# A recommendation network on one core: gathers without releases, three crossed tiles instead of four, a wait ahead of each one-hot, and fewer loads

## The chip, the cores and the metric

The kernel runs on one core of one Trainium2 chip. The metric is the device time of one execution, in microseconds (us). The kernel before takes 118.74 us, the median of three runs (118.56 to 119.22). The names of the engines are those of the profile: PE is TensorE's matmul, PEld its weight load, DVE is VectorE, ACT is ScalarE, POOL is GpSimd, SP is SyncE, which issues loads and stores here.

## The reference

For 2048 samples there are 13 dense numbers and eight indices. A wide part sums single weights, a deep part is a network of two hidden layers over eight embeddings of 64 numbers and a projection of the dense numbers. Cut to what matters:

```python
VOCABS = [125000, 25000, 12500, 375, 375, 1000, 500, 100]
wide = dense @ Wd_wide
for si, wi in zip(S, w):
    wide = wide + wi[si]
wide = wide + wc0[S[3] * VOCABS[4] + S[4]]
wide = wide + wc1[S[5] * VOCABS[6] + S[6]]
deep_in = concatenate([dense @ Wd_deep] + [Ei[si] for Ei, si in zip(E, S)], axis=1)
h = relu(deep_in @ W1)          # 576 -> 512
h = relu(h @ W2)                # 512 -> 256
deep = h @ W3                   # 256 -> 1
return bias + deep + wide
```

## The kernel before

**Tiling.** The samples are 16 tiles of 128, in four blocks (0 to 3) of four tiles, 512 samples each. Every float32 product with a weight is made of three matmuls on high and low parts (lines L891, L892, L893), so that layer 1 and layer 2 are most of PE's work.

**Two ways to fetch a row.** The three large tables (fields 0, 1, 2) are gathered: POOL issues one indirect DMA for each field and tile, into `x_pair` (fields 0 and 1, 32 gathers) and `x_two` (field 2, 16 gathers), and PE turns the rows over (`turn`, L856). The five small tables lie in SBUF. For them DVE builds a one-hot of each chunk of 128 rows (`build_onehot`, L556: 19 chunks a block, 128x512, float16 index against a row number, into `onehot`), and PE multiplies it with the table (`look_up`, L832) and with its single weights (`look_up_wide`, L844). The indices of a block come spread over all partitions: block 0 by matmuls, blocks 1 to 3 by a DMA (`idx_bc`, L323) from a copy stored in DRAM (`idx_dram`).

**The crossed weights.** `wc1` is gathered for all 16 tiles. `wc0` has 375 x 375 entries, and is gathered for the tiles from `XTILES` on, with 12 gathers (28 in all, `cross`, L388). For the first `XTILES` = 4 tiles PE multiplies a one-hot of the row with the table of 375 rows (`look_up_crossed`, L883, six matmuls of 376 columns), and DVE picks the column (`take_crossed`, L671). The table CROSSED says in which block and place each of these tiles stands on PE.

**Order.** Each engine's order is written by hand, and all waits are semaphores. PE's results of lookups, turns and crossed tiles go round three PSUM banks in the order of the list `IO_ORDER`; a use waits for the engines that empty the use three places earlier. POOL waits ahead of every gather but the first four (`gather_released`): PE counts its work in matmuls of 512 columns and releases gather after gather, one each 5.6 of them for the first eight, then one each 5.85 (`count`, `release_at`). Behind the 48 row gathers POOL issues the 28 of `cross`.

**The start.** SP issues the index, then tables and parts of W1, `look_w` (the single weights of the small tables), the dense numbers, the store of the indices, two parts of W1 and, once the store has landed, the spread of block 1. Behind that stand four small loads (`w3`, `bias`, `dense_s`, `wd_bc`) and then W2, whose buffer `w2_sb` is a part of `w1_sb`: it waits for the spread of block 1 and for `w1_low` (L334 to L337). ACT makes the high part of W2 (L484) ahead of `wide_looked(0)` and the lookups of block 1, and DVE its low part (L562) between the one-hots (1, 0) and (1, 1). Here and below (b, i) is block b and small table i. On PE the order there is `look_up(1, 0)`, `dense(0)`, `turn(0, 0)`, `look_up(1, 1)`, then the last part of block 0's layer 1 and layer 2.

**The end.** The last block's layers end on PE with L1000 and L1009. DVE adds the crossed weights once the last gather has landed (L784, L785), adds the last sums of PE (L788), and SP stores the result.

## Time and profile before

| | us |
|---|---|
| median of three runs | 118.74 |
| the profiled execution | 117.59 |
| its span, first to last instruction | 115.8 |
| PE busy in it | 110.4 |
| POOL busy in it | 84.7 |
| DVE busy in it | 73.1 |
| ACT busy in it | 57.2 |

The profile is of one execution, on one core. The span leaves out 1.8 us of that execution's time that lie around the instructions. Times in the rows below are from the span's start. An engine's busy time counts its instructions, not its issue of DMAs, except on POOL, where the making of a gather's descriptors is shown as an instruction (DMA_INDIRECT). Matmuls overlap, and the duration of one contains its passage through the array: two that follow each other start about 0.23 us apart, though each is shown with 0.39 us.

### The profile page before, as it was taken

How to read it: one execution, taken by the hardware profiler on the slowest of the kernel's cores; microseconds unless marked ns; L12 is line 12 of the kernel's file. 1: busy time of each engine (PE TensorE's matmuls, PEld its weight loads, DVE VectorE, ACT ScalarE, POOL GpSimd, SP SyncE). 2: the span in 40 equal slices, each digit the busy share in tenths (PEclk: the TensorE clock that was granted, in tenths of full speed). 3: DMA queues.
4: the chain of work that ended last, by engine and by line, in shares of the span. 5: the costliest groups of instructions: out<-in, count | busy, mean ns of one | idle time of the engine just before them, and what ended most of it. 6: DMA issues, size and time to landing. Idle time of an engine off the chain costs nothing.

```text
span 115.8 us, 1680 instructions
## 1 busy us (share of the span) xinstructions
PE 110.4 (95%) x572; PEld 85.2 (74%) x572; DVE 73.1 (63%) x186; ACT 57.2 (49%) x105; POOL 84.7 (73%) x87
## 2 busy tenths in 40 slices
PE   5999999979999999999999999999999999999980
PEld 2747685847787885888888886888888886888980
DVE  3699999287999955974992043992993024609211
ACT  5699992288785262249092251339273260426220
POOL 7574777765777977796777767777786777777750
PEclk9999999999999999999999999999999999999997
DMA  2798858348941143202335342320000000000000
GB/s 58 238 228 236 220 92 218 70 28 231 412 75 18 12 82 28 25 6 21 25 23 81 27 32 23 32 19 0 0 0 0 6 1 3 0 1 0 0 0 3
DMA packets 6168, 7.46 MB, mean 64 GB/s; under 512 B 2844, under 2 KB 3868, under 8 KB 6160
## 3 DMA queue, kind: packets, MB, share of 16 engines
q0 software_dynamic: 2432, 1.62, 17.2%
q1 hardware_dynamic: 3728, 5.74, 15.8%
q8 instruction: 4, 0.07, 0.2%
q14 instruction: 4, 0.03, 0.1%
HBM read 7.32 MB, written 0.03 MB: 63 GB/s over the span
## 4 chain that ended last, share of the span: by engine, by line
PE 72%; DMA 16%; SPq 4%; ACT 2%; POOL 2%; issue 1%; DVE 0%; DVEq 0%
PE l_ps L891 16%; PE l_ps L893 16%; PE l_ps L892 15%; PE io_ps L832 11%; DMA w_sb<-in_w_dram 5%; DMA idx_bc<-idx_dram 4%; DMA idx_dram<-row_idx 4%; PE io_ps L883 4%; PE io_ps L844 3%; PE l_ps L961 2%; DMA cross<-in_wc_dram,idx_cross 2%; PE io_ps L856 2%; POOL cross L388 2%; PE io_ps L986 2%; SPq L296 1%
## 5 line engine op out<-in xcount | busy, mean ns | idle before, releaser
L378 POOL DMA_INDIRECT x_pair<-in_rows_dram,idx_gather x32 | 35.2, 1100 | 12.3 <-issue 7.0
L388 POOL DMA_INDIRECT cross<-in_wc_dram,idx_cross x28 | 27.8, 992 | 8.5 <-issue 4.6
L556 DVE TENSOR_SCALAR onehot<-idx_bc,row_id 128x512 fp32r<-128x512 f16 x76 | 31.7, 482 | 2.2 <-PE io_ps L844 2.0
L378 POOL DMA_INDIRECT x_two<-in_rows_dram,idx_gather x16 | 19.6, 1228 | 5.9 <-issue 3.0
L891 PE MATMUL l_ps<-xt_hi,w_hi 128*128 128x512 f32 x56 | 22.3, 398 | 0.0
L893 PE MATMUL l_ps<-xt_hi,w_lo 128*128 128x512 f32 x56 | 22.0, 393 | 0.0
L892 PE MATMUL l_ps<-xt_lo,w_hi 128*128 128x512 f32 x56 | 21.9, 392 | 0.0
L832 PE MATMUL io_ps<-onehot,table_hl 128*128 128x512 f32 x76 | 21.2, 408 | 0.4 <-ACT xt_lo L417 0.4
L832 PEld LDWEIGHTS io_ps<-onehot,table_hl 128*128 128x128 f32 x76 | 14.1, 188 | 5.5 <-DVE onehot L556 1.6
L416 ACT CAST xt_hi<-io_ps 64x512 fp32r<-64x512 f32 x20 | 11.6, 579 | 12.0 <-PE io_ps L832 11.8
L610 DVE SCALAR_TENSOR_TENSOR h_lo<-l_ps,h_hi 128x512 fp32r<-128x512 f32 x16 | 10.1, 686 | 8.8 <-ACT h_hi L437 8.8
L446 ACT ACTIVATE h<-l_ps 128x512 f32<-128x512 f32 (+2 forms) x10 | 5.0, 512 | 19.3 <-PE l_ps L893 19.3
L891 PE MATMUL l_ps<-h_hi,w_hi 128*128 128x512 f32 (+1 forms) x36 | 13.4, 372 | 0.0
L893 PE MATMUL l_ps<-h_hi,w_lo 128*128 128x512 f32 (+1 forms) x36 | 13.3, 368 | 0.0
L892 PE MATMUL l_ps<-h_lo,w_hi 128*128 128x512 f32 (+1 forms) x36 | 13.2, 366 | 0.0
L891 PEld LDWEIGHTS l_ps<-xt_hi,w_hi 128*128 128x128 f32 x56 | 10.5, 188 | 2.7 <-issue 0.4
L577 DVE TENSOR_TENSOR xt_lo<-io_ps,xt_hi 128x512 fp32r<-128x512 f32 x4 | 2.8, 692 | 15.0 <-ACT xt_hi L430 15.0
L893 PEld LDWEIGHTS l_ps<-xt_hi,w_lo 128*128 128x128 f32 x56 | 10.5, 188 | 2.3
L892 PEld LDWEIGHTS l_ps<-xt_lo,w_hi 128*128 128x128 f32 x56 | 10.5, 188 | 2.3
L417 ACT CAST xt_lo<-io_ps 64x512 fp32r<-64x512 f32 x20 | 11.7, 583 | 0.5
L437 ACT ACTIVATE h_hi<-l_ps 128x512 fp32r<-128x512 f32 x16 | 8.7, 602 | 3.9 <-PE l_ps L893 3.6
L891 PEld LDWEIGHTS l_ps<-h_hi,w_hi 128*128 128x128 f32 x36 | 6.8, 189 | 1.4 <-issue 0.4
(106 smaller groups left out, 129.3 us busy)
## 6 DMA issues: line engine op xcount, KB each, us to landing
idx_bc<-idx_dram SPq DMA_DIRECT2D x3, 640.0 KB, 8.1
w_sb<-in_w_dram SPq DMA_DIRECT2D x4, 256.0 KB, 5.6
dense_x<-in_dense_x_dram SPq DMA_DIRECT2D x4, 154.0 KB
table<-in_wc_rows_dram SPq DMA_DIRECT2D x1, 564.0 KB, 6.0
x_pair<-in_rows_dram,idx_gather POOLq DMA_INDIRECT x32, 3.4
w_sb<-in_w_dram SPq DMA_DIRECT2D x1, 512.0 KB, 6.3
cross<-in_wc_dram,idx_cross POOLq DMA_INDIRECT x28, 2.4
x_two<-in_rows_dram,idx_gather POOLq DMA_INDIRECT x16, 3.6
```

What stands on the lines that cost most here:

```text
L378: nc.gpsimd.indirect_dma_start(out=x_two[:, t // 2, t % 2 * ROW:(t % 2 + 1) * ROW] if f == 2 else x_pair[:, t, f * ROW:(f + 1) * ROW], out ...
L388: nc.gpsimd.indirect_dma_start(out=cross[:, c, t:t + 1], out_offset=None, in_=wc[c], in_offset=bass.IndirectOffsetOnAxis(ap=idx_cross[:, c ...
L416: nc.scalar.copy(xt_hi[b % 2][to, g, :], bank[0:D, :]).then_inc(io_act, 1)
L417: nc.scalar.copy(xt_lo[b % 2][to, g, :], bank[D:2 * D, :]).then_inc(io_act, 1)
L437: nc.scalar.activation(h1_hi[:, m, :], l1_ps[m][:], ACT.Relu).then_inc(l1_high, 1)
L446: nc.scalar.activation(h2[:, m, s], l2_bank(part)[:, s], ACT.Relu).then_inc(h2_ready, 1)
L556: nc.vector.tensor_scalar(onehot[:, CHUNK0[i] + c, :], idx_bc[:, b % (BLOCKS - 1), i, :], row_id[:, c:c + 1], None, ALU.is_equal).then_inc ...
L610: nc.vector.scalar_tensor_tensor(out=h1_lo[:, m, :], in0=l1_ps[m][:], scalar=0.0, in1=h1_hi[:, m, :].bitcast(f32), op0=ALU.max, op1=ALU.su ...
L832: last = count(nc.tensor.matmul(io_bank(use)[:], table_hl[:, c, :], onehot[:, c, :], start=c == CHUNK0[i], stop=ends), free=not ends)
L891: count(nc.tensor.matmul(dst, w_hi, a_hi, start=start, stop=False), columns, free=True)
L892: count(nc.tensor.matmul(dst, w_hi, a_lo, start=False, stop=False), columns, free=True)
L893: return count(nc.tensor.matmul(dst, w_lo, a_hi, start=False, stop=stop), columns)
```

## The change

What it does:

- POOL waits for no release; PE counts no work and sends none.
- `XTILES` is 3: one crossed tile less on PE (that of block 2, ahead of `look_up_wide`) and on DVE, one matmul less in `spread_row`, and row one-hots of 384 columns where they had 512. POOL issues 29 gathers of `cross`, 77 in all.
- In `build_onehot`, DVE waits in blocks 1 to 3 ahead of each one-hot until the one before it is finished.
- In block 0 `look_up(0, 4)` comes ahead of `turn(0, 1)`, on PE and on ACT, and in IO_ORDER.
- `look_w`, `w3`, `bias`, `wd_wide` and `dense_s` come as one load, `few`, in the place of `look_w`.
- W2 has a buffer of its own, comes in rows of 4 KB laid out ahead, and is issued right behind the spread of block 1, without waits.

```diff
-XTILES = 4
+XTILES = 3
-PACE, FIRST_PACE, PACED_FROM = 5.85, 5.6, 9
-FIRST_RELEASED = BT * 2
-RELEASED = FIRST_RELEASED + (BLOCKS - 1) * BT * NG + NX * TILES - XTILES
-CROSSED = {(1, 3): [0], (2, 1): [1], (2, 3): [2], (3, 1): [3]}
+CROSSED = {(1, 3): [0], (2, 3): [1], (3, 1): [2]}
-IO_ORDER = [("look", 0, i) for i in range(4)] + [("turn", 0, 1), ("look", 0, 4), ("wide", 0, 0)]
+IO_ORDER = [("look", 0, i) for i in range(4)] + [("look", 0, 4), ("turn", 0, 1), ("wide", 0, 0)]
...
+        few = sb("few", [P, sum(FEW)], f32)
-        w2_sb = w1_sb[:, 2:4, :].rearrange("p g n -> p (g n)").rearrange("p (k n) -> p k n", n=H2)
+        w2_sb = sb("w2_sb", [P, M1, H2], f32)
...
-            sp.dma_start(look_w[:], small_w).then_inc(look_w_loaded, 16)
+            sp.dma_start(few[:], few_in).then_inc(few_loaded, 16)
...
             spread_block(1)
-            sp.dma_start(w3_sb[:], w3).then_inc(w3_loaded, 16)
-            sp.dma_start(bias_sb[:], bias.to_broadcast([P, 1])).then_inc(bias_loaded, 16)
-            sp.dma_start(dense_s[:], dense_s_in).then_inc(dense_s_loaded, 16)
-            sp.dma_start(wd_bc[:], wd_wide.to_broadcast([P, ND])).then_inc(wide_weight_loaded, 16)
-            sp.wait_ge(index_spread[1], 16)
-            sp.wait_ge(w1_low, 2)
-            sp.dma_start(w2_sb, w2.rearrange("(k p) n -> p k n", p=P)).then_inc(w2_loaded, 16)
+            sp.dma_start(w2_sb[:].rearrange("p k n -> p (k n)"), w2).then_inc(w2_loaded, 16)
             dense_block(1)
...
                         for f in fields:
-                            if b > 0 or f != 2:
-                                released += 1
-                                pool.wait_ge(gather_released, released)
                             nc.gpsimd.indirect_dma_start(
...
                 for c in every:
+                    if b > 0:
+                        dve.wait_ge(onehot_ready, b * NCH + CHUNK0[i] + c)
                     nc.vector.tensor_scalar(
                         onehot[:, CHUNK0[i] + c, :], idx_bc[:, b % (BLOCKS - 1), i, :], row_id[:, c:c + 1],
                         None, ALU.is_equal).then_inc(onehot_ready, 1)
...
             layer1(0, 2, range(2, M1))
+            look_up(0, 4)
             turn(0, 1)
-            look_up(0, 4)
             layer1_weights_low_last(3)
```

DVE's row in the start of block 1, where the waits for a one-hot come in; line numbers differ between the kernels, as the changed one is shorter. Before:

```order
L556 TENSOR_SCALAR onehot<-idx_bc,row_id 128x512 [waits io_full,index_spread1]
L556 TENSOR_SCALAR onehot<-idx_bc,row_id 128x512 x2
L562 TENSOR_TENSOR w_lo<-w_sb,w_hi 128x1024 [waits w2_high]
L556 TENSOR_SCALAR onehot<-idx_bc,row_id 128x512 x3
L577 TENSOR_TENSOR xt_lo<-io_ps,xt_hi 128x512 [waits io_act]
L556 TENSOR_SCALAR onehot<-idx_bc,row_id 128x512 x2
L610 SCALAR_TENSOR_TENSOR h_lo<-l_ps,h_hi 128x512 [waits l1_high] x4
L556 TENSOR_SCALAR onehot<-idx_bc,row_id 128x512 x3
```

And of the change:

```order
L535 TENSOR_SCALAR onehot<-idx_bc,row_id 128x512 [waits onehot_ready,io_full,index_spread1]
L535 TENSOR_SCALAR onehot<-idx_bc,row_id 128x512 [waits onehot_ready] x2
L541 TENSOR_TENSOR w_lo<-w_sb,w_hi 128x1024 [waits w2_high]
L535 TENSOR_SCALAR onehot<-idx_bc,row_id 128x512 [waits onehot_ready] x3
L556 TENSOR_TENSOR xt_lo<-io_ps,xt_hi 128x512 [waits io_act]
L535 TENSOR_SCALAR onehot<-idx_bc,row_id 128x512 [waits onehot_ready] x2
L587 SCALAR_TENSOR_TENSOR h_lo<-l_ps,h_hi 128x512 [waits l1_high] x4
L535 TENSOR_SCALAR onehot<-idx_bc,row_id 128x512 [waits onehot_ready] x3
```

The order is the same; each one-hot now waits for `onehot_ready`, its predecessor's own signal.

SP's row from `look_w` to the table of crossed weights. Before:

```order
L308 DMA look_w<-in_small_w_dram 128x19
L314 DMA dense_x<-in_dense_x_dram 77x512
L318 DMA idx_dram<-row_idx 80x128 [waits row_index_ready]
L299 DMA w_sb<-in_w_dram 128x512 x2
L323 DMA idx_bc<-idx_dram 128x2560 [waits row_index_stored]
L329 DMA w_sb<-in_w_dram 128x2
L330 DMA bias_sb<-in_bias_dram 128x1
L331 DMA dense_s<-in_dense_s_dram 128x208
L332 DMA wd_bc<-in_wd_wide_dram 128x13
L337 DMA w_sb<-in_w_dram 128x4x256 [waits w1_low,index_spread1]
L314 DMA dense_x<-in_dense_x_dram 77x512 [waits dense_split]
L344 DMA table<-in_wc_rows_dram 128x1128 [waits table_low,rows_gathered0_1,rows_gathered0_0]
```

And of the change:

```order
L298 DMA few<-in_few_dram 128x243
L304 DMA dense_x<-in_dense_x_dram 77x512
L308 DMA idx_dram<-row_idx 80x128 [waits row_index_ready]
L289 DMA w_sb<-in_w_dram 128x512 x2
L313 DMA idx_bc<-idx_dram 128x2560 [waits row_index_stored]
L319 DMA w_sb<-in_w_dram 128x1024
L304 DMA dense_x<-in_dense_x_dram 77x512 [waits dense_split]
L326 DMA table<-in_wc_rows_dram 128x1128 [waits table_low,rows_gathered0_1,rows_gathered0_0]
```

Four loads are gone between the spread (`idx_bc`) and W2 (`w_sb`, the 128x1024 one), with the two waits of W2.

PE's row in block 2, from the end of layer 1's part with pair 3 to `turn(2, 1)`. The name `x_two` marks that turn, `wide_deep_look` the turning of block 1's sums (`turn_deep(1)`). Before:

```order
L883 MATMUL io_ps<-cross_hl,row_onehot 128x376 [waits io_dve,io_act]
L883 MATMUL io_ps<-cross_hl,row_onehot 128x376 x5
L844 MATMUL io_ps<-onehot,look_w_parts 32x512 [waits io_dve,io_act]
L844 MATMUL io_ps<-onehot,look_w_parts 32x512 x18
L986 MATMUL io_ps<-ident,wide_deep_look 128x128 [waits io_dve,io_act,h2_used]
L986 MATMUL io_ps<-ident,wide_deep_look 128x128 x3
L856 MATMUL io_ps<-ident,x_two 128x128 [waits io_dve,io_act,rows_gathered2_1]
L856 MATMUL io_ps<-ident,x_two 128x128
```

And of the change:

```order
L805 MATMUL io_ps<-onehot,look_w_parts 32x512 [waits io_dve,io_act]
L805 MATMUL io_ps<-onehot,look_w_parts 32x512 x18
L943 MATMUL io_ps<-ident,wide_deep_look 128x128 [waits io_dve,io_act,h2_used]
L943 MATMUL io_ps<-ident,wide_deep_look 128x128 x3
L816 MATMUL io_ps<-ident,x_two 128x128 [waits io_dve,io_act,rows_gathered2_1]
L816 MATMUL io_ps<-ident,x_two 128x128
```

The crossed tile (L883, six matmuls) is gone ahead of `look_up_wide` (L844 and L805).

## Rows read from the trace of the kernel before

**Rows 1.** Page, part 1: engine, busy us, share of the span, instructions.
```profile
PE 110.4 (95%) x572; PEld 85.2 (74%) x572; DVE 73.1 (63%) x186; ACT 57.2 (49%) x105; POOL 84.7 (73%) x87
```

**Rows 2.** Busy time by stretch: us, busy us of each engine, granted clock, DMA share.
```profile
50.00:60.00 10.00, 10.00 (x46) 8.31 (x46) 7.61 (x19) 6.33 (x12) 8.17 (x7) 1.00 0.25 18
```

**Rows 3.** Timeline of the end: start us, us, engine, line, what.
```profile
111.88 0.58 PE L1009 MATMUL io_ps<-w_sb,h 128*128 128x1 f32 x4
...
111.07 0.94 POOL L388 DMA_INDIRECT cross<-in_wc_dram,idx_cross  x1 [0.30 <-issue]
...
113.42 0.17 DVE L784 TENSOR_TENSOR wide_cross<-wide_bias,cross 128x16 f32<-128x16 f32 x1 [2.56 <-DMA cross<-in_wc_dram,idx_cross]
...
113.72 0.15 DVE L788 TENSOR_TENSOR result<-wide_cross,io_ps 128x4 f32<-128x4 f32 x1
```

**Rows 4.** Chain of waits, in order of time: start us, us, what.
```profile
10.91 5.20 DMA idx_bc<-idx_dram
...
16.13 6.29 DMA w_sb<-in_w_dram
...
96.14 1.04 PE io_ps L883 x6
...
111.07 2.33 DMA cross<-in_wc_dram,idx_cross
```

**Rows 5.** Timeline of POOL: start us, us, what, idle before and who ended it.
```profile
3.83 1.10 POOL L378 DMA_INDIRECT x_two<-in_rows_dram,idx_gather  x1 [1.13 <-DVE idx_gather L541]
...
9.78 0.98 POOL L378 DMA_INDIRECT x_pair<-in_rows_dram,idx_gather  x1 [0.71 <-PE io_ps L832]
...
12.02 0.99 POOL L378 DMA_INDIRECT x_pair<-in_rows_dram,idx_gather  x1 [1.25 <-PE l_ps L891]
...
26.36 0.94 POOL L378 DMA_INDIRECT x_pair<-in_rows_dram,idx_gather  x1 [0.71 <-PE io_ps L832]
...
28.38 0.94 POOL L378 DMA_INDIRECT x_pair<-in_rows_dram,idx_gather  x1 [1.07 <-PE l_ps L891]
...
37.41 2.87 POOL L378 DMA_INDIRECT x_two<-in_rows_dram,idx_gather  x1 [0.30 <-issue]
...
48.54 3.70 POOL L378 DMA_INDIRECT x_pair<-in_rows_dram,idx_gather  x1 [0.30 <-issue]
...
76.01 1.28 POOL L388 DMA_INDIRECT cross<-in_wc_dram,idx_cross  x1 [0.30 <-issue]
...
106.01 0.94 POOL L388 DMA_INDIRECT cross<-in_wc_dram,idx_cross  x1 [0.30 <-PE l_ps L891]
```

**Rows 6.** Line L556, all its instructions: ns min/median/max.
```profile
L556 DVE TENSOR_SCALAR onehot<-idx_bc,row_id x76: 463/480/589, 4.9 to 85.9; 128x512 fp32r<-128x512 f16 x76
```

**Rows 7.** Timeline of DVE, starts and lengths in blocks 0 to 2.
```profile
32.24 0.19 DVE L536 SCALAR_TENSOR_TENSOR idx_wrap<-idx_pair,vocab 128x32 f32<-128x32 f32 x1
...
32.47 0.21 DVE L538 TENSOR_TENSOR idx_sum<-idx_wrap,idx_pair 128x32 f32<-128x32 f32 x1
...
35.70 3.26 DVE L556 TENSOR_SCALAR onehot<-idx_bc,row_id 128x512 fp32r<-128x512 f16 x8
...
48.17 3.25 DVE L556 TENSOR_SCALAR onehot<-idx_bc,row_id 128x512 fp32r<-128x512 f16 x8
```

**Rows 8.** Timeline of the start, ACT, DVE and PE.
```profile
22.44 1.05 ACT L484 CAST w_hi<-w_sb 128x1024 fp32r<-128x1024 f32 x1 [4.35 <-DMA w_sb<-in_w_dram]
...
23.52 1.23 DVE L562 TENSOR_TENSOR w_lo<-w_sb,w_hi 128x1024 fp32r<-128x1024 f32 x1 [2.67 <-ACT w_hi L484]
...
13.13 0.44 PE L856 MATMUL io_ps<-ident,x_two 128*128 128x128 f32 x2 [0.22 <-DMA x_two<-in_rows_dram,idx_gather]
...
24.21 0.66 PE L856 MATMUL io_ps<-ident,x_pair 128*128 128x128 f32 x4 [0.18 <-DMA x_pair<-in_rows_dram,idx_gather]
...
25.29 1.20 PE L832 MATMUL io_ps<-onehot,table_hl 128*128 128x512 f32 x3 [0.42 <-ACT xt_lo L417]
```

**Rows 9.** Timeline of PE, one lookup of eight chunks.
```profile
39.02 2.02 PE L832 MATMUL io_ps<-onehot,table_hl 128*128 128x512 f32 x8
```

More of the change, by code:

```diff
@@ L146, in program @@
         table_hl = sb("table_hl", [P, NCH, 2 * D], f32r)
-        look_w = sb("look_w", [P, NCH], f32)
+        few = sb("few", [P, sum(FEW)], f32)
+        look_w, w3_sb, bias_sb, wd_bc, dense_flat = (few[:, sum(FEW[:k]):sum(FEW[:k + 1])] for k in range(len(FEW)))
+        dense_s = dense_flat.rearrange("p (t k) -> p t k", k=ND)
         look_w_rest = sb("look_w_rest", [P, NCH], f32)
@@ L368, in _ @@
             pool.wait_ge(gather_index_ready, 1)
-            released = 0
             for b in range(BLOCKS):
@@ L831, in look_up @@
                     ends = c == CHUNK0[i] + CHUNKS[i] - 1
-                    last = count(nc.tensor.matmul(io_bank(use)[:], table_hl[:, c, :], onehot[:, c, :],
-                                                  start=c == CHUNK0[i], stop=ends), free=not ends)
+                    last = nc.tensor.matmul(io_bank(use)[:], table_hl[:, c, :], onehot[:, c, :],
+                                                  start=c == CHUNK0[i], stop=ends)
                 last.then_inc(io_full, 1)
```

105 lines of the change are left out of this document (38 added, 67 removed).

## The prediction, made before the changed kernel was run

> **What bounds the kernel now.** I read the page's first part, the busy time by stretch, the end of the timelines, the chain of waits, and then POOL, DVE and the start one by one. The page has PE busy for 95% of the span [rows 1], and the stretch from 50 to 60 us stands for all from 30 to 110 us: 10.00 of 10.00 us at the full granted clock, 2.4 GHz, while DVE and ACT have room [rows 2]. So whatever PE is spared in the middle comes off PE's end. The end itself is not PE's, though. PE's last matmul ends at 111.88 + 0.58 = 112.46 us, but the last gather, issued at 111.07, lands 2.33 us later, at 113.40 [rows 3, 4]. Only then DVE adds the crossed weights (L784, 113.42), and L788 closes at 113.72 + 0.15 = 113.87 [rows 3]. Two lines of work thus run side by side to the end, PE and POOL, and POOL is behind by 0.9 us. A gain on one alone is cut off by the other.
>
> **POOL's line, today.** From the first gather at 3.83 to the start of the last at 111.07 are 107.24 us for 75 steps [rows 3, 5]. An undisturbed step is 0.94 us of work and 0.30 us between, as at 106.01 [rows 5]; 75 of them are 93.0 us. The idle time before a gather that PE released is more than 0.30 in four places worth counting: 0.71, 1.25, 0.71 and 1.07 us, in sum 2.54 us over [rows 5]. After 30 us POOL hardly ever waits for a release: it runs behind them. What is left, 107.24 - 93.0 - 2.5 = 11.7 us, is gathers longer than 0.94 us. Two of them have 1.93 and 2.76 us of it (2.87 and 3.70 us, at 37.41 and 48.54), and both lie in a run of eight one-hots on DVE (35.70 to 38.96 and 48.17 to 51.42) [rows 5, 7]. In other such runs a gather is late by 0.34 us at most, as at 76.01 [rows 5]. So a gather can be kept out by one-hots that follow each other without a gap.
>
> **Releases gone, one gather more.** The removed waits give POOL 2.5 us, all of it ahead of 30 us, and the 77th gather costs 1.24 us. With the 11.7 us unchanged the last gather would start at 3.83 + 76 x 1.24 + 11.7 = 109.8, land at 112.1 and let DVE end 0.47 us later, at 112.6. That is 1.3 us before today's 113.87. For the gathers themselves being early does no harm: every one has its own place in `x_pair`, `x_two` or `cross`.
>
> **The wait ahead of each one-hot.** Today one takes 480 ns (463 to 589) [rows 6], and a run of eight takes 3.26 us [rows 7], so they start (3.26 - 0.48) / 7 = 0.40 us apart and overlap by 0.08. The trace has no one-hot that waits for its predecessor, but steps that do: L536 starts at 32.24 and takes 0.19, L538 starts at 32.47 [rows 7], 0.04 us after its end. So I take 0.48 + 0.04 = 0.52 us a one-hot, 0.12 us more. The bounds are 0 and 0.19 us (0.589 instead of 0.48, and the 0.04). Waits behind another instruction of DVE find the one-hot long finished and are free; 46 of the 57 follow a one-hot, so DVE does 5.5 us more in 80 us, and it has room. What is queued behind is the rest of DVE: low parts, row one-hots, the sums. PE waits for the one-hots themselves. The tightest place is (1, 4): 35.70, earlier by the 1.3 us below and later by three paid waits (0.37), is 34.8; the eighth one-hot is done at 34.8 + 0.48 + 7 x 0.52 = 38.9. PE's eighth matmul of that lookup, started today at 39.02 + 7 x 0.23 = 40.6 [rows 9], would want it at 39.3. So 0.4 us of cover are left there, and over 1 us at (2, 1) and (3, 1). I cost it at nothing for PE, and at 0.5 us as the outer bound.
>
> What it buys is the gap between two one-hots. If a stuck gather comes through with 0.34 us in place of 1.93 or 2.76 us, the two give 4.0 us back. Then POOL's line ends at 112.6 - 4.0 = 108.6. The bounds are 0 (the gap of 0.04 us is not enough) and 4.7 us. I take 4.0, since every other run of eight has its gathers at 0.34 us or less even without gaps. The Trainium skill (SBUF — State Buffer, in "SBUF: two separate sides") says of this that DVE and GpSimd take a shared pair of SBUF ports as an exclusive lock for a whole instruction, and that a software-made DMA then waits for its descriptors. The two long gathers agree with it; the other gathers in such runs, longer by 0.34 us at most, show that POOL needs the ports for a small part of its 0.94 us.
>
> **The crossed tile on PE.** Six matmuls of 376 columns: 1.04 us in the chain for one tile [rows 4], at full clock in a stretch with nothing idle. It was the only work between layer 1 and `look_up_wide` in block 2, and block 1 has gone without one there without a wait. The spread of three rows and not four spares one small matmul, about 0.05 us. Together 1.1 us off PE.
>
> **The start.** W2 is issued at 16.13 and is there 6.29 us later [rows 4]. ACT waits 4.35 us for it, and DVE 2.67 us for ACT [rows 8]; behind DVE's 1.23 us stand the one-hots (1, 1), so that PE starts `look_up(1, 1)` after an idle 0.42 us and gets its one-hots 0.40 apart (the record puts it to ACT, but DVE's first one-hot is what ends then). From the turn at 24.21 to the end of the lookup, 25.29 + 1.20 less the 0.16 us of passage, are 2.12 us for work of 1.15 (four half-size transposes 0.45, three matmuls 0.70). If W2 is there by 19, DVE makes the low part and the one-hots (1, 1) before PE gets there, and 0.95 us go. W2 is now issued at about 11.4, behind the spread of block 1 alone; its 6.29 us would end at 17.7, and up to 1.5 us later if the two share the engines. Next late is then the high part of `turn(0, 0)` on ACT, for 0.1 us. The wait of 0.22 us for `x_two` at 13.13 goes, because the lookup comes first, and its eight one-hots end soon enough; the wait of 0.18 us for `x_pair` at 24.21 [rows 8] goes, because the block's gathers are 0.41 + 0.95 us earlier [rows 5]. In all 0.95 + 0.22 + 0.18 - 0.1 = 1.25, say 1.3 us. Bounds: 0 and 1.6. `few` has the place of `look_w` and is some 120 KB where that was 10, which delays what is behind it by a few tenths; the first user of either comes at 15 us, and nothing of it is near.
>
> **The sum.** PE's last matmul ends at 112.46 - 1.1 - 1.3 = 110.1, DVE's L788 at 110.3, with POOL's line at 108.6 out of the way. Today's is 113.87: 3.6 us less, against the profiled execution's own 117.59 (span 115.8) a time of 114.0. The runs' median is 1.15 us above that execution. I take the difference over to it and round down: 118.74 - 3.5 = 115.2.
>
> **Rivals.**
> 1. POOL stays the bound. The gaps are too short, and the 11.7 us stay, or others get stuck in the 4.1 us runs. It decides as soon as those losses are above 110.3 - 100.9 = 9.4 us. With all of them the end is 112.6 and the time 118.74 - 1.3 = 117.4. For it speaks how short 0.04 us is, against it that most gathers in such runs pass even today with no gap at all. The last gather's landing would then end the chain again, PE being done 1 to 2 us before.
> 2. The start gives nothing. The spread of block 1 took 5.20 us with little beside it [rows 4]; with W2 right behind, both could slow down to 11.5 us in sum, W2 then lands at 22.4 as today, and only the crossed tile and POOL's 0.9 us are gained: 118.74 - 2.3 = 116.4. Against it: it takes a queue in which W2 moves only after everything else.
> 3. Slower than before: POOL holds DVE. In the gaps a gather gets in and keeps the next one-hot out for all of its 0.94 us. A run of eight meets three gathers, a run of three two. With a hold h, PE would wait 3h - 0.4 at (1, 4), 2h - 1.2 at (2, 1) and (3, 1) each, and 2h - 0.8 at (1, 1), in sum 9h - 3.6. With h = 0.94 that is 4.9 us and 118.74 - 3.5 + 4.9 = 120.1; it is slower than before from h = 0.79 on. Against it: of 76 one-hots, many of which start in the middle of a gather, none took over 589 ns [rows 6], so h is some 0.1 us. The rule of the Trainium skill named above, that whichever of the two starts first has the ports for the whole instruction, would give this rival if DMA_INDIRECT counted as one such instruction.
>
> **How the numbers follow.** The forecast has 0.60, POOL as the bound 0.18, the start without gain 0.15, DVE held 0.05, anything else 0.02. The range runs from 114.2 (all bounds on the good side: the start 1.6 us, and runs in which POOL was further behind than in the profiled one) to 117.2, which holds the second rival and most of the first. About 0.5%, 0.6 us, is what a measurement can tell from no change. Faster by more than that: 0.91; within it, mostly from the first rival with more losses or the third with a small hold, 0.05; slower 0.04.
>
> **What would show it.** In the profile of the changed kernel: the last gather landed 1 to 2 us before PE's last matmul, and L788's counterpart right behind PE; no gather over 1.5 us in blocks 1 to 3; runs of eight one-hots at 4.1 us; W2's high part on ACT ahead of 20 us, with no idle PE between 13 and 26 us; 18 matmuls with a crossed tile, not 24. Wrong would be a PE that idles ahead of a lookup in block 1 for a one-hot, or a chain that ends in a gather.

## The result, and the profile after

The changed kernel takes **115.02 us** (median of 4 runs, 114.75 to 115.29), the kernel before 118.65 us (median of 4, 117.99 to 119.22). The ratio is 0.970, with a 95% interval of 0.964 to 0.975: faster by 3.6 us, against 3.5 forecast. Here and below a ratio counts only runs within 1.5% of the fastest of their kernel, while medians and ranges count all of them.

The page of the changed kernel, engines and chain (part 1: busy us, share of the span, instructions; part 4: shares of the chain that ended last):

```profile
span 113.5 us, 1658 instructions
...
PE 109.7 (97%) x565; PEld 84.5 (74%) x565; DVE 79.9 (70%) x184; ACT 57.1 (50%) x105; POOL 80.1 (71%) x88
...
PE 91%; ACT 3%; DMA 2%; DVE 1%; issue 1%
```

PE's share is up from 95 to 97%, and DVE has 6.8 us more work than in [rows 1]. Now the end, by the chain of waits (start us, us, what):

```profile
110.13 0.79 PE io_ps L957 x8
110.92 0.46 PE io_ps L967 x4
...
111.41 0.16 DVE result L762
```

and by the tile `cross`, which the last gathers write (the first row gives ns min/median/max and first and last start; the last one the time from issue to landing):

```profile
L364 POOL DMA_INDIRECT cross<-in_wc_dram,idx_cross x5: 940/944/944, 99.2 to 104.2; - x5
...
L758 DVE TENSOR_TENSOR wide_cross<-wide_bias,cross x1: 169/169/169, 109.7 to 109.7; 128x16 f32<-128x16 f32 x1
...
DMA to landing us min/median/max: 2.3/2.4/2.4
```

The last gather is issued at 104.2, not 111.07 [rows 3], and lands by 106.6. DVE adds the crossed weights at 109.7, as soon as it gets to them, and then waits for PE alone. The chain of [rows 4] that ended in a gather is gone. The last operation of DVE starts 0.05 us after PE's last matmul ends (110.78 + 0.58 = 111.36); in [rows 3] it started 1.26 us after. The end moved from 113.87 to 111.41 + 0.16 = 111.57, so this profiled execution (115.29 us) is 2.3 us shorter than the one before (117.59), while the medians are 3.6 us apart. Of the 2.3 us, 1.2 are that POOL is no longer behind, and 1.1 that PE ends earlier. The difference between 2.3 and 3.6 is taken up below.

DVE in blocks 1 and 2, the rows that answer to [rows 7]:

```profile
35.21 4.61 DVE L535 TENSOR_SCALAR onehot<-idx_bc,row_id 128x512 fp32r<-128x512 f16 x8
...
44.95 1.53 DVE L535 TENSOR_SCALAR onehot<-idx_bc,row_id 128x512 fp32r<-128x512 f16 x3 [1.37 <-issue]
...
47.79 4.88 DVE L535 TENSOR_SCALAR onehot<-idx_bc,row_id 128x512 fp32r<-128x512 f16 x8
```

and the line itself, to be held against [rows 6] (ns min/median/max, and who waited for it, us and times):

```profile
L535 DVE TENSOR_SCALAR onehot<-idx_bc,row_id x76: 474/487/697, 4.9 to 85.8; 128x512 fp32r<-128x512 f16 x76
...
who waited for it (us, times):
  PEld io_ps L793: 1.0, 2
```

A run of eight takes 4.6 to 4.9 us, not 3.26. POOL's timeline shows what that buys. These are all the gathers over 1.4 us:

```profile
12.38 1.88 POOL L356 DMA_INDIRECT x_pair<-in_rows_dram,idx_gather  x1 [0.30 <-issue]
...
14.57 1.80 POOL L356 DMA_INDIRECT x_pair<-in_rows_dram,idx_gather  x1 [0.30 <-issue]
...
21.91 1.90 POOL L356 DMA_INDIRECT x_pair<-in_rows_dram,idx_gather  x1 [0.30 <-issue]
...
68.56 1.46 POOL L364 DMA_INDIRECT cross<-in_wc_dram,idx_cross  x1 [0.30 <-issue]
```

The gathers of 2.87 and 3.70 us [rows 5] have no counterpart. The sum of what the gathers take above 0.94 us, called POOL's losses from here on, fell from 11.1 us to 5.5 us. Three of the four above lie ahead of 24 us. Two of these are in block 0, whose one-hots carry no wait. The other two of the four stand beside a single DVE instruction, where a wait between one-hots can't help: the one at 21.91 beside the low part of W2 (21.78, 1.21 us, below), the one at 68.56 beside an operation on `wide_deep_look` (L603, 68.46, 0.74 us). Both gathers end 0.82 us after that instruction does.

The start, rows that answer to [rows 8]:

```profile
12.43 0.43 SPq L319 DMA_DIRECT2D w_sb<-in_w_dram  x1
...
18.53 1.05 ACT L460 CAST w_hi<-w_sb 128x1024 fp32r<-128x1024 f32 x1
...
21.78 1.21 DVE L541 TENSOR_TENSOR w_lo<-w_sb,w_hi 128x1024 fp32r<-128x1024 f32 x1
...
13.45 2.09 PE L793 MATMUL io_ps<-onehot,table_hl 128*128 128x512 f32 x8 [0.33 <-ACT xt_lo L393]
...
24.64 0.94 PE L793 MATMUL io_ps<-onehot,table_hl 128*128 128x512 f32 x3
```

W2 is issued at 12.43 us, an us later than forecast, and early enough: neither ACT nor DVE waits for it any more, and the three-chunk lookup at 24.64 starts without a wait. An idle 0.33 us ahead of the eight-chunk lookup at 13.45 is new.

### The profile page after: what moved, and what is told of

Read it like the earlier page. It is cut to its first block, busy times and chain, and to the rows that moved or that the text cites. A ratio compares the mean times of both kernels' runs of the same rounds, so it can differ in the third digit from the quotient of the medians.

```text
span 113.5 us, 1658 instructions
## 1 busy us (share of the span) xinstructions
PE 109.7 (97%) x565; PEld 84.5 (74%) x565; DVE 79.9 (70%) x184; ACT 57.1 (50%) x105; POOL 80.1 (71%) x88
## 4 chain that ended last, share of the span: by engine, by line
PE 91%; ACT 3%; DMA 2%; DVE 1%; issue 1%
PE l_ps L848 18%; PE l_ps L850 18%; PE l_ps L849 18%; PE io_ps L793 15%; PE io_ps L805 4%; PE l_ps L918 3%; PE io_ps L842 3%; PE io_ps L816 2%; DMA idx_raw<-in_index_dram 2%; PE l_ps L881 2%; PE l_ps L777 2%; PE io_ps L943 2%; ACT xt_lo L393 1%; ACT xt_hi L392 1%; PE l_ps L989 1%; PE l_ps L885 1%
## 5 line engine op out<-in xcount | busy, mean ns | idle before, releaser
L535 DVE TENSOR_SCALAR onehot<-idx_bc,row_id 128x512 fp32r<-128x512 f16 x76 | 39.3, 532 | 5.1 <-issue 2.8
L356 POOL DMA_INDIRECT x_pair<-in_rows_dram,idx_gather x32 | 34.2, 1069 | 9.7 <-issue 9.7
L793 PE MATMUL io_ps<-onehot,table_hl 128*128 128x512 f32 x76 | 20.7, 405 | 0.3 <-ACT xt_lo L393 0.3
L356 POOL DMA_INDIRECT x_two<-in_rows_dram,idx_gather x16 | 15.8, 986 | 5.8 <-issue 4.6
L422 ACT ACTIVATE h<-l_ps 128x512 f32<-128x512 f32 (+2 forms) x10 | 5.0, 512 | 20.2 <-PE l_ps L850 20.2
L848 PEld LDWEIGHTS l_ps<-xt_hi,w_hi 128*128 128x128 f32 x56 | 10.5, 188 | 2.8 <-issue 0.5
L850 PEld LDWEIGHTS l_ps<-xt_hi,w_lo 128*128 128x128 f32 x56 | 10.5, 188 | 2.5
L393 ACT CAST xt_lo<-io_ps 64x512 fp32r<-64x512 f32 x20 | 11.7, 583 | 0.5
L556 DVE TENSOR_TENSOR xt_lo<-io_ps,xt_hi 128x512 fp32r<-128x512 f32 x4 | 2.8, 692 | 11.8 <-ACT xt_hi L406 11.8
```

The source lines that it names most:

```text
L356: nc.gpsimd.indirect_dma_start(out=x_two[:, t // 2, t % 2 * ROW:(t % 2 + 1) * ROW] if f == 2 else x_pair[:, t, f * ROW:(f + 1) * ROW], out ...
L393: nc.scalar.copy(xt_lo[b % 2][to, g, :], bank[D:2 * D, :]).then_inc(io_act, 1)
L422: nc.scalar.activation(h2[:, m, s], l2_bank(part)[:, s], ACT.Relu).then_inc(h2_ready, 1)
L535: nc.vector.tensor_scalar(onehot[:, CHUNK0[i] + c, :], idx_bc[:, b % (BLOCKS - 1), i, :], row_id[:, c:c + 1], None, ALU.is_equal).then_inc ...
L793: last = nc.tensor.matmul(io_bank(use)[:], table_hl[:, c, :], onehot[:, c, :], start=c == CHUNK0[i], stop=ends)
L848: nc.tensor.matmul(dst, w_hi, a_hi, start=start, stop=False)
```

## The experiments

Three questions: which edit gives what, whether edits that look separate depend on each other, and why PE got a little slower per matmul, which nothing in the prediction foresaw. The runs were made in five further sessions on four chips (the second and the fourth session had the same chip), and each kernel is compared with the kernel before in its own session. The changed kernel itself ran in the third alone, so times and traces that are set against it from the fourth and fifth come from different chips. In the first two sessions the kernel before took 129 to 130 us, in the other three about 117. These three come first.

### Both kernels' halves: releases back, waits out, waits alone

Third session. The changed kernel again, as a base for this chip:

> The changed kernel once more, unchanged, beside the kernel before on the same chip. In its first measurement it took 115.0 us against 118.65; on two other chips the kernel before took 129 to 130 us, and every kernel that gathers without releases 184 to 190, PE standing still until POOL's last gather. Theory A, it depends on the chip or its state and on the releases: if the kernel before takes 128 us or more here, this one takes 180 to 190; if the kernel before takes 118 to 119, this one takes 115. Theory B, only the variants had that fault and the change itself does not: 115 to 125 whatever the kernel before takes.

Measured: 115.26 us (114.88 to 115.75), the kernel before 116.80, ratio 0.991 (0.983 to 0.998). The last gather is issued at 104.45, POOL's losses are 6.0 us, DVE's last operation waits for PE at 111.14. So the traces repeat to 0.3 us, but the gain here is 1% (1.1 us by the ratio), not 3%: it is the kernel before that differs between sessions. The kernel before took neither the 118 to 119 us nor the 128 that the first theory has as its conditions; the changed kernel took the 115 us that go with the former.

The changed kernel with the releases of its 73 gathers put back (waits, three tiles and loads kept):

```diff
                         for f in fields:
+                            if b > 0 or f != 2:
+                                released += 1
+                                pool.wait_ge(gather_released, released)
                             nc.gpsimd.indirect_dma_start(
```

> The changed kernel with the releases of the kernel before put back (same count of work, 73 releases), its tiles, waits, order and loads as changed. Theory A, a release keeps POOL from running ahead of a PE that stands still: on a chip where the kernel before takes 128 to 130 us this one takes 122 to 126, not 180; on a chip where that one takes 118.65, this takes 115 to 116, since POOL's 2.5 us of waits are covered by the 4 to 5 us that POOL's line was ahead in the changed kernel's trace. Theory B, another part of the change makes PE stand still: 180 or more here too. Step of PE's matmuls: 0.2295 us if it hangs on the releases, 0.2332 if on another part.

Measured on the same chip: 117.23 us (116.65 to 118.49), level with the kernel before (ratio 1.006, 0.996 to 1.016), and by the two ratios about 1.7 us more than the changed kernel. The expectation, 115 to 116 us with the releases covered, missed. Its PE, POOL and DVE at the end:

```profile
110.84 0.58 PE L997 MATMUL io_ps<-few,h 128*128 128x1 f32 x4
...
110.08 0.94 POOL L377 DMA_INDIRECT cross<-in_wc_dram,idx_cross  x1 [0.30 <-PE l_ps L879]
...
112.56 0.18 DVE L771 TENSOR_TENSOR wide_cross<-wide_bias,cross 128x16 f32<-128x16 f32 x1 [2.71 <-DMA cross<-in_wc_dram,idx_cross]
```

The losses are as low as without releases (5.4 us, a gather of 2.07 us at 33.28 among them), and still the last gather is issued 5.6 us later. PE's last matmul ends at 110.84 + 0.58 = 111.42, 0.3 us later than in the changed kernel beside it (111.10), and DVE's last operation, L775, starts at 112.85, not at 111.46 where PE would let it. So of the 1.7 us between the two profiled executions (116.74 and 115.03) 1.4 are POOL's wait. The step from matmul to matmul stays that of the changed kernel, so it doesn't hang on the releases.

Fourth session. The other half, the kernel before with nothing but the waits:

```diff
                 for c in every:
+                    if b > 0:
+                        dve.wait_ge(onehot_ready, b * NCH + CHUNK0[i] + c)
                     nc.vector.tensor_scalar(
```

> The kernel before with the one-hot waits of blocks 1 to 3 alone, releases and loads kept. Theory (waits open room for POOL's gathers, PE is not held by them): POOL's losses between gathers fall from 11 to about 4.5 us and none is stuck for over 2.2 us in blocks 1 to 3, but the releases, which PE sets at its own pace, still bind the last gather, so it is issued at 110.5 to 111 on an undisturbed chip as before, and the time falls by no more than 1 us against the kernel before. Rival (the stuck gathers were the whole loss): the last gather comes 2 to 4 us earlier and the time is 2 to 3% down, as with the whole change. Second rival (waits hold PE): 1 us slower.

Measured: 116.34 us (115.63 to 118.28), the kernel before 117.70 (115.52 to 121.62, 19 runs), ratio 1.003 (0.995 to 1.010): no change. The losses halve (5.3 us), but the last gather moves by only 2.0 us against the trace of [rows 3], and DVE still waits for it:

```profile
111.19 0.58 PE L1012 MATMUL io_ps<-w_sb,h 128*128 128x1 f32 x4
...
109.04 1.02 POOL L388 DMA_INDIRECT cross<-in_wc_dram,idx_cross  x1 [0.30 <-issue]
...
111.50 0.17 DVE L787 TENSOR_TENSOR wide_cross<-wide_bias,cross 128x16 f32<-128x16 f32 x1 [1.33 <-DMA cross<-in_wc_dram,idx_cross]
```

The theory's part on POOL and on the time both held; the last gather came earlier, by 1.5 us, than the 110.5 to 111 I had expected. Part of that is PE, which sets the releases and reached layer 2 at 28.33 here, 0.9 us earlier than in the other trace. And the wait for the gather costs nothing here: DVE's last operation (L791, 111.81) starts 0.04 us after PE's last matmul ends (111.77). The two lines are level.

And the changed kernel without its waits, on the same chip:

```diff
-                    if b > 0:
-                        dve.wait_ge(onehot_ready, b * NCH + CHUNK0[i] + c)
```

> The changed kernel without its one-hot waits; releases still gone. Prediction's theory: the waits buy 4.0 us of POOL's losses, so here the losses are back near 11 us, with the two stuck gathers; the last gather is issued at about 108 instead of 104.2, lands before PE's last matmul or up to 0.5 us behind it, and the time is 0 to 1 us over the changed kernel's. Rival from the two disturbed chips: gathers that nobody releases let PE stand still while they run, and the waits hide it; then this kernel stands near 185 to 190 us on this chip too, with PE's gaps in the records put down to issue.

Measured: 116.81 us (114.90 to 120.19, 4 runs), too scattered for an interval. The rival, 185 us or more, is out here. Now the profile of the run of 115.63 us. The losses are back at 10.5 us, two gathers are stuck in runs of eight (49.36, 2.01 us and 58.05, 1.68 us) and one (33.27, 2.10 us) beside DVE's low part of `cross_hl`, a single instruction of 1.33 us. POOL is level with PE again at the end:

```profile
111.05 0.58 PE L964 MATMUL io_ps<-few,h 128*128 128x1 f32 x4
...
108.71 1.27 POOL L364 DMA_INDIRECT cross<-in_wc_dram,idx_cross  x1 [0.30 <-issue]
...
111.43 0.17 DVE L755 TENSOR_TENSOR wide_cross<-wide_bias,cross 128x16 f32<-128x16 f32 x1 [1.38 <-DMA cross<-in_wc_dram,idx_cross]
```

DVE's last operation (L759) starts at 111.73, 0.10 us after PE's last matmul ends (111.63), where the changed kernel has 0.05. So in this execution the waits would have bought no more than 0.06 us of time. The four runs took 114.90, 115.63 (the trace), 117.98 and 120.19 us; no trace shows what the last two lost. On an undisturbed chip the waits are thus shown to halve POOL's losses, and not to shorten the time.

The four together, start of the last gather and POOL's losses, each from its profile:

| | no waits | waits |
|---|---|---|
| releases | 111.07, 11.1 us (before, 76 gathers) | 109.04, 5.3 us (76); 110.08, 5.4 us (77) |
| no releases | 108.71, 10.5 us (77) | 104.16, 5.5 us; 104.45, 6.0 us (77) |

Taking 75 or 76 undisturbed steps of 1.24 us and the losses from the whole, what is left is waiting for releases: 107.24 - 93.0 - 11.1 = 3.1 us in the kernel before, 105.23 - 93.0 - 5.3 = 6.9 us with the waits added (first gather at 3.81). In the changed kernel, which has no releases, 0.5 us are left (100.21 - 94.2 - 5.5), so this sum is that much too high. A POOL that loses less only runs into the releases sooner. The waits alone move the last gather by 2.0 us, the releases alone by 2.4, or 3.6 at equal count of gathers; both move it by 8.2 at equal count. The rows come from different chips, and where there are releases PE's own start is in them, so differences of a few tenths say nothing.

### The step from matmul to matmul

Grouped by line and shape, 56 matmuls each (busy us, mean ns of one), the changed kernel:

```profile
L848 PE MATMUL l_ps<-xt_hi,w_hi 128*128 128x512 f32 x56 | 22.5, 402 | 0.0
L849 PE MATMUL l_ps<-xt_lo,w_hi 128*128 128x512 f32 x56 | 22.1, 395 | 0.0
L850 PE MATMUL l_ps<-xt_hi,w_lo 128*128 128x512 f32 x56 | 22.1, 395 | 0.0
```

The same groups of the kernel before:

```profile
L891 PE MATMUL l_ps<-xt_hi,w_hi 128*128 128x512 f32 x56 | 22.3, 398 | 0.0
L893 PE MATMUL l_ps<-xt_hi,w_lo 128*128 128x512 f32 x56 | 22.0, 393 | 0.0
L892 PE MATMUL l_ps<-xt_lo,w_hi 128*128 128x512 f32 x56 | 21.9, 392 | 0.0
```

It is only 2 to 4 ns, but it is in every profile of the changed kernel and its variants, with and without releases, with and without waits, at the same granted clock. Their starts are 0.2332 us apart on the mean, and 0.2295 in those of the kernel before. One candidate is left by the diff: `few` and an own `w2_sb` move every later tile to another SBUF address (`xt_hi`, `xt_lo`, `h1_hi` and `h1_lo` by 3776 bytes a partition, `w1_hi` by -256, `w2_hi` by 3840). So the changed kernel was laid out as before, with gaps (fourth session):

```diff
-        few = sb("few", [P, sum(FEW)], f32)
+        sb("gap_look_w", [P, NCH], f32)
...
+        few = sb("few", [P, sum(FEW)], f32)
+        sb("gap_rest", [P, 40], f32)
         wd_rep = sb("wd_rep", [D, NROWS], f32)
...
-        w2_sb = sb("w2_sb", [P, M1, H2], f32)
...
+        sb("gap_w3_bias", [P, 16], f32)
         x_pair = sb("x_pair", [P, TILES, 2 * ROW], f32)
...
         result = sb("result", [P, TILES], f32)
+        w2_sb = sb("w2_sb", [P, M1, H2], f32)
```

> The changed kernel, with gaps put between its tiles in SBUF so that the operands of the layers and of the one-hot matmuls (one-hots, tables, transposed rows, hidden values, weights) lie at the very addresses that they had in the kernel before; few stands where the dense inputs were and w2_sb behind the last tile. Question: a 512-column matmul of the layers follows the last one after 0.2332 us in every profile of the changed kernel and its variants, and after 0.2295 us in those of the kernel before. Theory A, addresses: the step is back at 0.2295, PE's last matmul comes 1.3 to 1.6 us earlier than in the changed kernel (at about 109.3 instead of 110.8 on an undisturbed chip), and the time is 1 to 1.5 us under that of the changed kernel, unless POOL's last gather then ends it. Theory B, the step hangs on something else of the program (its instructions, its order): 0.233, and the changed kernel's time.

Measured: 114.36 us (114.07 to 115.45, 10 runs; ratio to the kernel before 0.987, 0.981 to 0.992). The groups read:

```profile
L851 PE MATMUL l_ps<-xt_hi,w_hi 128*128 128x512 f32 x56 | 22.3, 398 | 0.0
L853 PE MATMUL l_ps<-xt_hi,w_lo 128*128 128x512 f32 x56 | 22.0, 393 | 0.0
L852 PE MATMUL l_ps<-xt_lo,w_hi 128*128 128x512 f32 x56 | 21.9, 392 | 0.0
```

These are the kernel before's numbers, so the addresses set the step: theory A. What it is worth I had put too high: I had counted 480 matmuls with this step, and the traces have about 250 pairs of layer matmuls that follow each other directly. The stretch from the first matmul of layer 2 to the first of its last group has the same work in both, in the changed kernel

```profile
28.50 0.47 PE L848 MATMUL l_ps<-h_hi,w_hi 128*128 128x512 f32 x1
...
104.34 0.40 PE L848 MATMUL l_ps<-h_hi,w_hi 128*128 128x512 f32 x1
```

and with the old addresses

```profile
27.88 0.47 PE L851 MATMUL l_ps<-h_hi,w_hi 128*128 128x512 f32 x1
...
103.20 0.39 PE L851 MATMUL l_ps<-h_hi,w_hi 128*128 128x512 f32 x1
```

that is 75.84 against 75.32 us. So the addresses cost 0.5 us by this pair. The kernel before takes 105.47 - 29.20 = 76.27 us for the stretch, with one crossed tile more; 76.27 - 1.1 = 75.2, and by that it is 0.65 us. Which tile's address does it was not tried.

### Fewer crossed tiles

Fourth session as well. If PE alone bounds the changed kernel, a tile less on it should give its 1.1 us again:

```diff
-XTILES = 3
+XTILES = 2
-CROSSED = {(1, 3): [0], (2, 3): [1], (3, 1): [2]}
+CROSSED = {(1, 3): [0], (2, 3): [1]}
```

> The changed kernel with two crossed tiles on TensorE instead of three: 78 gathers instead of 77 on POOL, 1.1 us less on PE (12 transposes and matmuls of one tile). Theory (PE bounds the changed kernel alone, POOL has room: its last gather is issued at 104.2 and lands about 3 us before PE's last matmul): PE's last matmul 1.1 us earlier, time 1.0 to 1.2 us (0.9%) under the changed kernel's. Rival (another gather is what ends it): the last gather's landing moves from 106.5 to 107.8, still before PE, so no change or slower only if PE is held by gathers, as on the two disturbed chips, where it would be near 190.

Measured: 114.05 us (113.68 to 114.75; ratio 0.987, 0.978 to 0.996). The stretch of layer 2 (28.10 to 102.97) is 74.87 us, 1.0 less than the 75.87 of the changed kernel run again (28.21 to 104.08). The last gather is issued at 105.65, and DVE adds the crossed weights at 108.33 without a wait. The theory held, both on PE and on POOL; the time is 1.2 us under the changed kernel's of the third session.

Fifth session. Both at once, two tiles and the old addresses:

> The changed kernel with two crossed tiles on TensorE and with the addresses of the kernel before, both at once. Theory (the two gains are independent, both are PE's): the step is 0.2295 us, PE's last matmul comes 1.2 us earlier than with two tiles alone (at about 108.2 instead of 109.41), the last gather is issued at 105.6 and lands at about 108.1 to 108.3, still before it, and the time is 112.6 to 113.0 us on an undisturbed chip, about 1% under each of the two changes alone. Rival (POOL's line is next: its last gather lands at 108.3 and two DVE operations follow it): the gain of both together is cut off and the time stays at 113.4 or above, with DVE's crossed sum waiting for the gather.

Measured: **113.38 us** (113.08 to 114.50, 6 runs), the kernel before 117.29, ratio 0.974 (0.967 to 0.982): the fastest version here, though missing the 112.6 to 113.0 expected. Its rows:

```profile
28.66 0.47 PE L851 MATMUL l_ps<-h_hi,w_hi 128*128 128x512 f32 x1
...
102.89 0.39 PE L851 MATMUL l_ps<-h_hi,w_hi 128*128 128x512 f32 x1
...
108.19 0.17 DVE L761 TENSOR_TENSOR wide_cross<-wide_bias,cross 128x16 f32<-128x16 f32 x1
...
109.92 0.16 DVE L765 TENSOR_TENSOR result<-wide_cross,io_ps 128x4 f32<-128x4 f32 x1 [1.35 <-PE io_ps L970]
```

The stretch of layer 2 takes 74.23 us, 0.64 less than with two tiles alone, so the gains do add. DVE does not wait for a gather, so the rival is out. In the profiled execution (113.80) what is missing was lost ahead of 28.66: it came to layer 2 0.56 us later than the one of two tiles alone. Whether that holds for the other five runs isn't shown.

### Two sessions in which PE stood still

First session, on a chip where the kernel before took 130.09 us (128.06 to 130.70):

> The kernel before once more, unchanged, for a second trace. Its profiled execution took 117.59 us where its unprofiled median is 118.65, and in its trace two layer matmuls start 0.2295 us apart where in the changed kernel's trace they start 0.2332 apart, which over some 480 columns-of-512 matmuls is 1.5 us of the span. Theory A, the step belongs to the execution and not to the program: this trace has a step near 0.2332 and a span near 117. Theory B, the change slows PE (POOL or DVE being busier beside it): this trace has 0.2295 again and a span of 115.8. On POOL's line, the theory of stuck gathers expects two or more gathers over 1.9 us in other places than 37.41 and 48.54, since it is a matter of chance which of them meets a run of one-hots.

> Only one part of the change: the wait ahead of each one-hot of blocks 1 to 3. Theory of two lines (the end is the later of PE's last matmul and the last gather's landing): POOL's losses fall by about 6 us (in the changed kernel's trace they are 5.4, before 11.2), so POOL is no longer behind and PE's last matmul, at 112.5 to 114 depending on the step of its matmuls, ends the chain. The time falls by 0.9 to 1.5 us, to about 117.4. Rival, the waits do nothing for the end because POOL is held back by the releases of PE: 118.6 as before. Rival, the waits cost PE: one-hot runs of eight at 4.8 us delay the lookup (1, 4) and the time rises to 119 or more.

> The changed kernel without the waits ahead of one-hots, all else as changed. Theory of two lines: gathers get stuck again; with POOL's losses at 11 to 12 us its last gather lands at 112 to 113 us, behind PE's 111.4, and the time is 115.6 to 116.8. With another two or three stuck gathers it is more, and it varies more from run to run than the changed kernel's 114.75 to 115.29. Rival, waits are irrelevant and the gain is all PE's (tile, loads): 115.0 or, as DVE is spared 7 us, a little under.

> The changed kernel with one crossed tile on PE in place of three; two gathers more on POOL. Theory of two lines: PE's last matmul comes 2 x 1.04 + 0.1 us earlier, at 109.2, POOL's last gather starts 2 x 1.25 us later, at 106.7, and lands at 109.0. Both lines are even, and the time falls by 2.0 to 2.2 us, to 112.9. Rival, something else sets the end in the changed kernel (DVE's sums, the load of weights): less than 1 us. If POOL loses more than in the changed kernel's trace, it becomes the bound again: 113.5 to 114.

None of the times expected of these four could be tested, since what follows sets every time here. The kernel before measured 129.9 us. Its gathers are stuck beside the same two runs of eight as before (2.87 us at 37.73, 3.69 us at 51.09), where I had expected other places and chance, and its losses are 11.0 us. Its step is 0.2296 us, so the step does not belong to one execution. But its PE stopped for 5.20 us ahead of 78.87 with nothing to wait for. With the waits alone it took 125.59 us (124.99 to 129.64), ratio 0.975 (0.956 to 0.995), losses 4.5 us. Both kernels without releases fell apart: the changed kernel without waits took 188.69 us (183.84 to 189.26), the one with a single crossed tile, waits kept, 189.88 (188.82 to 190.81). Busy time by stretch of the kernel without waits (us; busy us and instructions of PE, PEld, DVE, ACT, POOL; granted clock; DMA share; GB/s):

```profile
60.00:80.00 20.00, 0.00 (x0) 0.00 (x0) 0.00 (x0) 0.51 (x2) 15.12 (x17) 0.50 0.18 13
...
120.00:140.00 20.00, 20.00 (x92) 16.36 (x91) 11.74 (x27) 8.85 (x16) 0.00 (x0) 1.00 0.02 8
```

PE has no instruction on record in 20 us in which POOL issues its gathers at an even pace. The trace puts PE's 26 us of idling ahead of 80.14 down to ACT's L422, and that one waited 32 us for something that the trace doesn't resolve. Some matmul records can be missing, so who stood still first isn't certain here. POOL's last gather is issued at 103.25. PE goes on with one matmul in 2.80 us until 108.18, and from 114 us on it is busy without a gap again. To see whether releases are what it hangs on, the kernel before without them, in the second session (the kernel before 128.84 us, 127.78 to 130.63):

```diff
-                            if b > 0 or f != 2:
-                                released += 1
-                                pool.wait_ge(gather_released, released)
```

> Only one part of the change: the kernel before with no release of gathers, neither the waits on POOL nor the signals on PE's matmuls. In the earlier runs the kernel before took 130 us and the two variants of the changed kernel 189 us, on a chip on which PE stood still for microseconds with nothing recorded that it waits for; the kernel before with waits ahead of one-hots had 126 us there. Theory A, unreleased gathers are what PE's standstills hang on: on such a chip this kernel takes 180 us or more. Theory B, they hang on another part of the change (the loads, the order of the start): it stays near 130 us there. On a chip without standstills, the theory of two lines expects POOL's line 2.5 us earlier: 117.2 to 118.0 against 118.65, the end being PE's or POOL's by chance. On the step of PE's matmuls: 0.2332 us if it hangs on the releases (as in the changed kernel's trace), 0.2295 if not.

Measured: 186.15 us (162.12 to 189.49). The timeline of PE at 80 to 90 us:

```profile
83.79 0.58 PE L956 MATMUL l_ps<-dense_hl,wdense_hl 77*128 77x512 f32 x1 [2.22 <-issue]
86.59 0.58 PE L956 MATMUL l_ps<-dense_hl,wdense_hl 77*128 77x512 f32 x1 [2.21 <-issue]
89.39 0.58 PE L956 MATMUL l_ps<-dense_hl,wdense_hl 77*128 77x512 f32 x1 [2.21 <-issue]
```

One matmul each 2.80 us, at a granted clock of 0.50 (1.2 GHz; on the page it is full until PE's busy share has dropped from nine tenths to three), while POOL goes on every 1.25 us. In the fourth session the same chip ran the changed kernel without waits in 114.90 to 120.19 us. So this is a condition that comes and goes, not a property of a program or of a chip. While it lasts, all three kernels without releases that were tried took 57 to 60 us more than the kernel before (by medians; one run of this last one only 33 us more), which itself took about 12 more than in the other sessions. The unmodified changed kernel was never run in it, though a variant with waits and one tile was. What stops PE's issue there isn't shown by these records. What they show is that in the second session taking out the releases alone brought it on, and that PE's step of 2.80 us ends about 5 us after the issue of POOL's last gather (issued at 103.25 and at 103.49, last such step to 108.18 and to 108.98 in the two traces above).

## Why the prediction was right, and where only its sum was

**Two lines of work, a gain on one alone cut off: right, but closer than I had it.** The last gather held the end back by 1.2 us in the kernel before and by 1.4 us in the changed kernel with its releases put back. With only one of the two edits on POOL's line the lines came out level: PE ends the kernel with the waits alone, and the gather is 0.06 us behind PE without the waits. Only both edits give POOL the 5 us of room in which a crossed tile can come off PE and be a gain.

**Releases, 2.5 us: right alone, wrong beside the waits.** At equal count of gathers they gave 3.6 us without waits: some 3 us of waiting for releases, and losses that came out 0.6 us smaller. But I added 2.5 and 4.0 us as if independent, and wrote that after 30 us POOL hardly ever waits for a release. That held only while POOL lost 11 us. With the losses halved the releases would have cost 6.9 us. Together the edits gave 8.2 us, not 6.5, and the last gather was issued at 104.16 where I had 105.8. On the time this had no effect, POOL being 5 us ahead.

**What the waits buy, 4.0 us of losses: right on POOL, wrong in time.** They bought 4.5 to 5.0 us (10.5 against 5.5 and 6.0). But I had put all of it on two gathers in runs of eight. Without waits and without releases two sit so, with 1.1 and 0.7 us over 0.94; the rest is that 14 gathers are over 1.2 us there, and 5 in the changed kernel. Nor are waits a cure for all: with releases put back a gather of 2.07 us stands at 33.28, beside the same `cross_hl` instruction, which has no gap in it. The kernel before had one there too (33.87, 1.93 us), which I left out of the account of the 11.7 us. In time I had the waits at 112.6 - 110.3 = 2.3 us. Without them POOL's line ended at 111.88 in the trace and PE's not at 110.1 but at 111.63, so nothing was left for them to gain there.

**What a wait costs, 0.12 us: right for the wait, missed for the gathers.** A run of three, 1.53 us, has a pitch of (1.53 - 0.49) / 2 = 0.52, as forecast. A run of eight has (4.61 - 0.49) / 7 = 0.59 to 0.63. A wait of 0.04 us is thus right, and on top come gathers that now get in between: the longest one-hot is 697 ns, not 589. This is the third rival's hold h, with 0.2 us at most instead of its 0.94, far under the 0.79 from which it decides. So the two engines do not treat each other alike: a gather waits for the end of a DVE instruction, or of a run of them, and a one-hot does not wait for the end of a gather. PE had the cover I named: it never stood idle for a one-hot; the 1.0 us in the row above is weight loads'.

**The crossed tile, 1.1 us: right.** One tile less gave 1.0 us of the stretch of layer 2 in the experiment.

**The start, 1.3 us: of the W2 part the size is open, the rest wrong.** From the lookup of the wide part to layer 2, the kernel before needs 29.20 - 18.10 = 11.1 us, the changed one 28.50 - 18.50 = 10.0, and every one of its variants 9.96 to 10.0. That looks like the forecast 0.95 + 0.18 - 0.1. But the trace of the kernel before with the waits alone has the old loads too, and needs 28.33 - 17.96 = 10.4. There W2 came sooner, and PE waited for no one-hot behind it:

```profile
20.79 1.05 ACT L484 CAST w_hi<-w_sb 128x1024 fp32r<-128x1024 f32 x1 [2.40 <-DMA w_sb<-in_w_dram]
```

So the new loads give 1.1 us against an execution in which W2 is late (22.44, [rows 8]) and 0.4 against one in which it is not; no run has the loads as its only change. And the 0.22 us ahead of it did not show in the time: layer 2 was reached 0.7 us earlier, not 1.3, since the wide part now began at 18.50 and not 18.10. There the chain runs through ACT, whose second table part waited 0.32 us for its DMA and whose copies were 0.3 to 0.5 us late from then on. In its variants that wide part began between 17.92 and 18.78, and at 17.96 in the kernel before with waits alone, so it is the scatter of the start more than an effect of the edit. I had called these tenths harmless because nothing near needs `few`; the tenths were in the loads ahead of it.

**What no step foresaw: 0.65 us for the addresses.** I read the diff for what it moves in time, not in memory. PE's last matmul was to end at 110.1 and ended at 110.78 + 0.58 = 111.36: later by 1.2 us, of which 0.65 are the addresses and 0.6 the start.

**Why the number was right all the same: luck.** On the profiled executions I forecast 3.6 us and 2.3 came. On medians 3.5 were forecast and 3.6 came. The kernel before was profiled in an execution 1.15 us under its median, the changed kernel in one 0.27 us above. I carried the difference over unchanged, and the 1.4 us happened to make up for what the two steps above missed. In the third session the same two kernels were 1.1 us apart by the ratio. Why the kernel before takes 118.65 us in one session and as little as 115.5 in single runs of others isn't shown; W2 being late, as in its trace, is one candidate, and no run tests it.

## What to carry to other kernels

Two limits on one engine's queue, here releases and stuck gathers, must be costed together: what one removes, the other takes over, and a sum of single gains is wrong in either direction. Compare where tiles lie before and after a change, because two loads put into new tiles moved every later operand and cost PE 0.5% without an instruction more. And before a brake is taken off, try the kernel on more than one chip and at more than one time: the brake that cost 1.7 us in one condition saved 57 in another.

## What the runs showed of the hardware

- The same 512-column matmuls follow each other 0.2332 or 0.2295 us apart, by the SBUF addresses of the kernel's tiles alone, at the same granted clock.
- A gather by indirect DMA was held back by up to 2.76 us in a run of eight one-hots on DVE without gaps, and, in blocks 1 to 3 of the changed kernel, by 0.5 us at most, where each one-hot waited for its predecessor and began about 0.04 us after its end; the one-hots were in turn held by 0.2 us at most.
- A late gather goes by the end of a DVE instruction. In the nine traces of the undisturbed sessions 145 gathers after the first took 1.04 us or more, and 137 of them ended 0.81 to 0.84 us or 0.11 to 0.14 us after a DVE instruction's end (2.87 us at 37.41 and 3.70 us at 48.54 in the kernel before: 0.12 us after a row one-hot, 0.82 us after the last of the eight). It depends on the instruction. Where DVE was busy with a low part of W1 or W2 (`w_lo`, both inputs in SBUF) from 0.06 to 0.26 us after the gather's start, all 29 gathers were late; where it was busy with `h_lo` (one input in PSUM), none of 68 was; with a one-hot, 47 of 215.
- In two sessions PE stood still (5.20 us ahead of 78.87 in the kernel before) or issued one matmul in 2.80 us, with nothing in the records to wait for, while POOL issued gathers; without releases this went on as long as POOL issued them every 1.25 us, and for about 5 us after, at a granted clock of 0.50. In three others the same kernels, or ones like them, ran at 113 to 117 us.
